# Router columns inside the first up unit's matmul group, and 12 of 64 recurrence slots as one instruction

## The chip, the cores and the metric

One core of one Trainium2 chip runs the whole program. The metric is the device time in microseconds (us) from the start to the end of one execution. The engines are TensorE (PE; its weight loads are listed apart as PEld), VectorE (DVE), ScalarE (ACT), GpSimd (POOL) and SyncE (SP), which only issues DMAs here.

## The reference

An image batch x of shape (8, 192, 16, 16) is taken as 8 sequences of 256 tokens with 192 channels. It passes two residual blocks:

```python
x = x + conv_ref(_ln_c(x), Wq, Wk, Wv, Wb, Wo)   # t = ln(x); returns t + delta_rule(...) @ Wo
t = tokens(x); t = t + ffn_ref(_ln_t(t), ...)
```

The first block is a delta rule with 12 heads of size 16. For each token, S is a 16x16 state per head, and with k and q normalised to length one

```
u_t = beta_t * (v_t - S_{t-1}^T k_t);  S_t = S_{t-1} + k_t u_t^T;  o_t = S_t^T q_t
```

The second block is a mixture of experts: a router gives 8 logits, of whose softmax the two largest are kept and normalised; each expert is silu(x @ w_gate) * (x @ w_up) @ w_down with a hidden size of 192, and a shared expert of hidden size 768 is mixed in by alpha = sigmoid(x @ sg_w + sg_b). All data are fp32.

## The kernel before, in words

**Chunks.** The 256 tokens of each sequence are cut into 16 chunks of T = 16 tokens; a chunk of 8 sequences has 128 tokens, one for each partition. All engines run the same outer loop `step(c)` for c from -3 to 18, and each writes out by hand, in one list for c < 1, one for 1 <= c < 16 and one for the rest, in which order it does its parts. `at(d, fn)` does the part fn for chunk c + d, so a step holds work of up to seven chunks:

- stage A of chunk c + 3 and c + 2 (norm, q, k, v projections, their silu and norms, splitting of k in a high and a low part, a trip through DRAM that lays k and q out for the recurrence),
- the recurrence of chunk c on DVE, with k rows put into PSUM by `fill(c, f)` on PE, two tokens at a time,
- `reading` and `summing` of chunk c on POOL: the products of states and q (`PQ`), half a chunk at a time, and their sums (`oT`),
- stage Fa of chunk c - 1: `Fa_otok` on DVE, `Fa_o` and `Fa_y` on PE (output projection and residual), norm, `Fa_h`, `Fa_hT` (the normed tokens transposed, high parts in `hiT`), `Fa_split` (low parts in `loT`), router logits, gates,
- stage Fb of chunks c - 1 and c - 2: 12 up units (8 experts, 4 quarters of the shared one). `Fb_up(n)` is five fp32r matmuls of 384 columns into one of two PSUM banks; ACT's `unit` makes `sg` (silu) and `ug` (times the gate) of them, POOL's `hidden` multiplies the two (`hid`), PE turns them by `Fb_turn(g)` in five groups, ACT copies them to `hidT`, `Fb_down(g)` multiplies them with the down weights,
- stage Fc of chunk c - 3 writes the output.

**The recurrence.** Each of a chunk's 16 tokens i takes four slots, 4i to 4i + 3: `Pr` = S * k (line 1301), `u` = minus the sum over a row of `Pr` (line 1303), k * u in place in PSUM (line 1305), and the new state `SH` (line 1309). In each slot a helper `each` issues the same operation twice, for the branches `br` 0 and 1 (six heads each, 128x96 elements); each branch waits for its own result of the slot before. Behind every slot `others(slot)` issues whatever small operations are hung on this slot by `at(slot, d, fn)`: stage A's and Fa's DVE parts and, at slots 48 to 58, the choice of the two experts (`Fa_max`, `G_dif`, ... `G_gate`).

**Router.** `Fa_logits` on PE is a plain fp32 product of `h2T` (an fp32 copy of the normed tokens, made by the last two of `Fa_hT`'s five ACT copies) with `Wr0`, `Wr1` into bank 1. DVE and ACT read the logits there.

**Start.** SP and ACT issue the loads of all weights. ACT and POOL split the up weights (`raw0`, `raw1`) into high and low parts in 12 pieces each (`weights_hi0`, `weights_lo0`, `weights_hi1`, `weights_1`). POOL's memsets come first of all; DVE builds `Sel` from `ident` after them, and PE waits for `Sel`.

## Time and profile before

| what | value |
|---|---|
| median of three runs | 497.47 us (497.37 to 498.15) |
| profiled execution, its own time | 497.98 us |
| its span, first to last instruction | 496.2 us |
| DVE busy | 428.0 us, 86% |
| PE busy | 425.9 us, 86% |
| POOL busy | 414.0 us, 83% |
| ACT busy | 349.7 us, 70% |

A busy share is the union of an engine's instructions over the span. The times in all rows count from the span's start. The steady part, chunks 2 to 12, lies between about 87 and 375 us; before it are the loads and the first chunks, behind it the last chunks and, from about 451 us on, the feed-forward work of the last two chunks.

### The profile page before, as it was taken

How to read it: one execution, taken by the hardware profiler on the slowest of the kernel's cores; microseconds unless marked ns; L12 is line 12 of the kernel's file. 1: busy time of each engine (PE TensorE's matmuls, PEld its weight loads, DVE VectorE, ACT ScalarE, POOL GpSimd, SP SyncE). 2: the span in 40 equal slices, each digit the busy share in tenths (PEclk: the TensorE clock that was granted, in tenths of full speed). 3: DMA queues.
4: the chain of work that ended last, by engine and by line, in shares of the span. 5: the costliest groups of instructions: out<-in, count | busy, mean ns of one | idle time of the engine just before them, and what ended most of it. 6: DMA issues, size and time to landing. Idle time of an engine off the chain costs nothing.

```text
span 496.2 us, 10722 instructions
## 1 busy us (share of the span) xinstructions
PE 425.9 (86%) x2464; PEld 391.3 (79%) x2464; DVE 428.0 (86%) x2546; ACT 349.7 (70%) x1039; POOL 414.0 (83%) x527
## 2 busy tenths in 40 slices
PE   0344276899999999999999999999999989899996
PEld 0233144789999989899898989898988979898996
DVE  2349989999999999999999999999999999997200
ACT  2795445686878787877778686878786848385763
POOL 5288699989899999999999898998999999896341
PEclk9855555999999999999999999999999999999999
DMA  7948373543323222323233332323222323200300
GB/s 203 223 100 159 94 180 100 111 103 111 79 68 88 72 78 74 92 65 102 68 84 87 81 89 78 89 72 83 80 83 74 83 78 86 81 28 0 114 2 16
DMA packets 44752, 44.12 MB, mean 89 GB/s; under 512 B 19920, under 2 KB 36496, under 8 KB 44688
## 3 DMA queue, kind: packets, MB, share of 16 engines
q1 hardware_dynamic: 40944, 40.87, 32.3%
q10 hardware_dynamic: 3744, 2.57, 1.8%
q8 instruction: 20, 0.33, 0.3%
q14 instruction: 44, 0.36, 0.2%
HBM read 37.13 MB, written 6.29 MB: 87 GB/s over the span
## 4 chain that ended last, share of the span: by engine, by line
DVE 73%; PE 11%; SPq 4%; issue 3%; POOL 3%; DMA 3%; ACT 2%; DVEq 0%; ACTq 0%; POOLq 0%
DVE Pr L1301 16%; DVE u L1303 15%; DVE bank L1305 15%; DVE SH L1309 12%; PE bank L427 2%; DMA k_scratch<-khl 2%; DVE st L1041 2%; SPq L249 2%; SPq L214 1%; DVE ss L1116 1%; PE bank L412 1%; DVE mv L1042 1%; DVE otok L1148 1%; DVE loT L1084 1%; PE bank L400 1%
## 5 line engine op out<-in xcount | busy, mean ns | idle before, releaser
L931 POOL TENSOR_TENSOR hid<-sg,ug 128x192 f32<-128x192 f32 x192 | 112.3, 608 | 23.0 <-ACT ug L669 21.4
L886 POOL TENSOR_TENSOR PQ<-SH,QB 128x768 f32<-128x768 f32 x62 | 112.5, 1835 | 5.8 <-DVE SH L1309 5.8
L1301 DVE TENSOR_TENSOR Pr<-SH,bank 128x96 f32<-128x96 f32 x512 | 104.8, 245 | 4.3 <-PE bank L361 3.9
L893 POOL TENSOR_TENSOR PQ<-PQ 128x768 f32<-128x768 f32 (+2 forms) x93 | 103.3, 1111 | 6.0
L1305 DVE TENSOR_TENSOR bank<-bank,u 128x96 f32<-128x96 f32 x512 | 106.5, 252 | 0.0
L427 PE MATMUL bank<-Wd,hidT 128*128 128x192 f32 x576 | 106.4, 326 | 0.0
L1303 DVE TENSOR_REDUCE u<-Pr 128x6 f32<-128x102 f32 x512 | 105.9, 247 | 0.0
L1309 DVE TENSOR_TENSOR SH<-SH,bank 128x96 f32<-128x96 f32 x512 | 103.0, 241 | 0.0
L427 PEld LDWEIGHTS bank<-Wd,hidT 128*128 128x128 f32 x576 | 95.3, 190 | 0.0
L668 ACT ACTIVATE sg<-bank 128x192 f32<-128x192 f32 x192 | 63.0, 328 | 45.0 <-PE bank L404 25.7
L361 PE MATMUL bank<-KR,Sel 128*128 128x384 f32 x128 | 58.3, 460 | 22.0 <-DVE SH L1309 12.5
L400 PE MATMUL bank<-Whi,hiT 128*128 128x384 f32 x192 | 72.2, 376 | 0.7 <-ACT ug L669 0.7
L404 PE MATMUL bank<-W,loT 128*128 128x384 f32 x192 | 65.3, 340 | 0.0
L402 PE MATMUL bank<-Whi,loT 128*128 128x384 f32 x192 | 65.3, 340 | 0.0
L403 PE MATMUL bank<-W,hiT 128*128 128x384 f32 x192 | 65.1, 339 | 0.0
L401 PE MATMUL bank<-Wlo,hiT 128*128 128x384 f32 x192 | 65.1, 339 | 0.0
L679 ACT ACTIVATE hidT<-bank 128x512 f32<-128x512 f32 (+1 forms) x80 | 44.3, 554 | 14.6 <-PE bank L412 12.8
L669 ACT ACTIVATE ug<-bank,gate 128x192 f32<-128x192 f32 x128 | 53.4, 417 | 0.0
L412 PE MATMUL bank<-ident,hid 128*128 128x128 f32 x288 | 45.7, 277 | 7.6 <-ACT hidT L679 7.5
L703 ACT ACT_TABLE_LOAD x38 | 48.8, 1283 | 0.7
L361 PEld LDWEIGHTS bank<-KR,Sel 128*128 128x128 f32 x128 | 25.9, 204 | 27.7 <-DVE SH L1309 16.6
L412 PEld LDWEIGHTS bank<-ident,hid 128*128 128x128 f32 x288 | 33.8, 141 | 12.4 <-issue 10.7
(150 smaller groups left out, 836.6 us busy)
## 6 DMA issues: line engine op xcount, KB each, us to landing
QB<-q_scratch SPq DMA_DIRECT2D x64, 384.0 KB
k_scratch<-khl SPq DMA_DIRECT2D x64, 48.0 KB, 1.7
KR<-k_scratch SPq DMA_DIRECT2D x32, 96.0 KB, 2.4
q_scratch<-qn SPq DMA_DIRECT2D x64, 24.0 KB, 1.6
Wd<-in_L_ffn_w_down_dram SPq DMA_DIRECT2D x4, 288.0 KB, 8.0
out_dram<-xT SPq DMA_DIRECT2D x1, 896.0 KB, 5.2
Wlo_unsplit<-in_L_ffn_w_gate_dram ACTq DMA_DIRECT2D x1, 768.0 KB, 5.6
Wlo_unsplit<-in_L_ffn_w_up_dram ACTq DMA_DIRECT2D x1, 768.0 KB, 8.8
```

The source lines that it names most:

```text
L361: mm(bKB[f % 2][:, 0:2 * BR * G], Sel[:, f].rearrange("p b x e -> p (b x e)"), KR[:, p, :], start=True, stop=True).then_inc(s_fill, 1)
L400: mm(to, hiT[:, p, 0:P], Whi0[:, n], start=True, stop=False)
L402: mm(to, loT[:, p, 0:P], Whi0[:, n], start=False, stop=False)
L412: last = tr(bHt[:, (k - lo) * P:(k - lo + 1) * P], hid[:, k % (KT // 2) * P:(k % (KT // 2) + 1) * P], ident[:, :])
L427: last = mm(bDn[:, 0:C], hidT[:, turn_half(g), k - lo, :], Wd[:, k, :], start=False, stop=(k == KT - 1))
L886: tt(PQ[:, at * BR * HP:(at + n) * BR * HP].rearrange("p (i b h) d -> p i b (h d)", i=n, b=BR), SH[:, lo:lo + n].rearrange("p i b h d -> p ...
L893: chained(tt(PQ[:, :, 0:w], PQ[:, :, 0:w], PQ[:, :, w:2 * w], ALU.add))
L931: tt(hid[:, r * H:(r + 1) * H], sg[:, m % RING], ug[:, m % RING], ALU.mult).then_inc(s_hid, 1)
L1301: v = each(lambda br: count(tt(Pr[:, br, i, :, 0:D], prev[:, br], KB[:, br], ALU.mult)), Sb)
L1303: v = each(lambda br: count(nc.vector.tensor_reduce(u[:, i % 2, br], Pr[:, br, i], X, ALU.add, negate=True)), v)
L1305: v = each(lambda br: count(tt(KB[:, br], KB[:, br], u[:, i % 2, br].unsqueeze(2).to_broadcast([P, HP, D]), ALU.mult)), v)
L1309: ins = tt(SH[:, i, br], prev[:, br], KB[:, br], ALU.add)
```

## The change

1. The router's columns stand ahead of unit 0's in the split weights. `Whi0`, `Wlo0` and `W1` get R = E + 2 = 10 columns in front (8 router columns and the shared gate's twice). `Fb_up(0)` multiplies 394 columns instead of 384; the logits are its columns 0 to 8 in `bUp[0]`. `Fa_logits`, `h2T` and its two copies, `Wr0` and `Wr1` go. DVE's `Fa_max` and ACT's `Fa_exp` read `bUp[0]`. Nine DMAs on SP load the router's columns instead of four.
2. In chunks 1 to 15, the slots of `WHOLE` (12 of 64) issue one instruction of 128x192 for both branches instead of two of 128x96; it waits for both.
3. `rstd_1` = 1 + rstd, a DVE operation in `A_bias`, becomes `A_plus` on ACT.
4. Waits at the start are moved: DVE's first wait for the memsets of `loT` and `hlo` goes to `A_low`, PE's wait for `Sel` to the first `fill`.
5. The written-out orders of PE, ACT, POOL and DVE are new. In both versions all 12 gated products of a chunk are done by POOL (`hidden`).

```diff
+R = E + 2
+WHOLE = frozenset((28, 32, 37, 38, 49, 50, 51, 54, 55, 56, 57, 58))
+        def columns(n):
+            return slice(0 if n == 0 else R + n * 2 * H, R + (n + 1) * 2 * H)
...
-                sp.dma_start(Wr0[:, 0:E], router_w[0:C0, :]).then_inc(s_wr, 16)
...
+                load_router(sp, 0, raw0[:, :], 0, C0)
+                load_router(sp, 1, raw1[0:C1], C0, C)
+                load_router(sp, 1, raw1[C1:P], C0, C)
...
-            def Fa_logits(f, p):
...
             def Fb_up(f, p, n):
-                to = bUp[n % 2][:, 0:2 * H]
-                mm(to, hiT[:, p, 0:P], Whi0[:, n], start=True, stop=False)
...
+                w = columns(n)
+                to = bUp[n % 2][:, 0:w.stop - w.start]
+                mm(to, hiT[:, p, 0:P], Whi0[:, w], start=True, stop=False)
...
             # PE, 1 <= c < 16
                     at(-1, Fa_h)
+                    at(-2, Fb_turn, 2)
+                    at(0, fill, 6)
                     at(-2, Fb_up, 11)
+                    at(-1, Fb_up, 0)
                     at(-2, Fb_down, 0)
-                    at(0, fill, 6)
-                    at(-1, Fa_logits)
-                    at(-2, Fb_turn, 2)
                     at(0, fill, 7)
-                    at(-1, Fb_up, 0)
+                    at(-2, Fb_down, 1)
                     at(-1, Fb_up, 1)
-                    at(-2, Fb_down, 1)
+                    at(1, fill, 0)
+                    at(-2, Fb_down, 2)
                     at(-2, Fb_turn, 3)
                     at(3, A_h)
...
             # ACT
+            def A_plus(a, p):
+                f(rstd_1[:, :], rstd1, ACT.Identity, bias=one[:, 0:1]).then_inc(s_plus, 1)
...
                 f(hiT[C1:P, p, P:2 * P], bFa[0:C1, P:2 * P], ACT.Copy)
-                f(h2T[:, 0:P], bFa[:, 0:P], ACT.Copy)
-                f(h2T[0:C1, P:2 * P], bFa[0:C1, P:2 * P], ACT.Copy).then_inc(s_h2T, 1)
...
                     at(-2, unit, 11)
+                    table(c + 2, LN_EXP)
+                    at(2, A_inv)
                     table(c - 1, LN_EXP)
                     at(-1, Fa_exp)
-                    table(c + 2, LN_EXP)
-                    at(2, A_inv)
                     table(0, SILU)
...
             # DVE
-                plus = count(ts(rstd_1[:, :], rstd1, 1.0, None, ALU.add))
-                dve.wait_ge(*plus)
...
             def Fa_max(q, p):
-                dve.wait_ge(s_lg, q + 1)
+                dve.wait_ge(s_up, q * UN + 1)
...
-                        at(8, 2, A_low)
-                        at(19, 2, A_z)
+                        at(7, 2, A_low)
+                        at(17, 2, A_z)
                         at(23, -1, Fa_otok)
-                        at(26, 3, A_stats)
-                        at(30, 3, A_var)
-                        at(30, 1, A_vT)
-                        at(31, -1, Fa_stats)
-                        at(31, -1, Fa_var)
-                        at(35, -1, Fa_bias)
-                        at(39, 3, A_bias)
-                        at(45, -1, Fa_split)
-                        at(46, 2, A_ss)
+                        at(27, 3, A_stats)
+                        at(28, 1, A_vT)
+                        at(31, 3, A_var)
+                        at(32, -1, Fa_stats)
+                        at(32, -1, Fa_var)
+                        at(36, -1, Fa_bias)
+                        at(37, 2, A_ss)
+                        at(38, 3, A_bias)
+                        at(43, -1, Fa_split)
                         at(48, -1, Fa_max)
...
-                            for br in range(BR):
-                                if waits[br] is not None:
-                                    dve.wait_ge(*waits[br])
-                                got.append(fn(br))
+                            for lo in range(BR) if c < 1 or slot not in WHOLE else (0,):
+                                hi = lo + 1 if c < 1 or slot not in WHOLE else BR
+                                for need in dict.fromkeys(made[lo:hi]):
+                                    if need is not None:
+                                        dve.wait_ge(*need)
+                                got += [fn(lo, hi)] * (hi - lo)
```

The other order changes that the text speaks of: POOL does `A_qn` before `A_vn` and `A_kn` and behind `hidden` 11; on ACT `A_h` and `A_xh` come behind the second table load, `unit` 1 ahead of `hidden` 3, and the last pieces `weights_hi1` behind `Fa_oc`; on PE `A_qk` comes ahead of `fill` 2 and `A_vb` behind it.

## Rows read from the trace of the kernel before

**Rows 1.** The page: the chain that ended last, shares of the span by engine.
```profile
DVE 73%; PE 11%; SPq 4%; issue 3%; POOL 3%; DMA 3%; ACT 2%; DVEq 0%; ACTq 0%; POOLq 0%
```

**Rows 2.** One steady chunk: busy us (count) of PE, PEld, DVE, ACT, POOL; clock; DMA.
```profile
237.28:263.41 26.13, 25.32 (x156) 23.88 (x155) 25.93 (x160) 20.51 (x64) 24.16 (x31) 1.00 0.31 81
```

**Rows 3.** The chain in order of time (start, us, what): one operation per chunk.
```profile
106.27 0.45 DVE ss L1116
...
367.92 0.45 DVE ss L1116
```

**Rows 4.** DVE's timeline in a steady chunk (start, us, line, operation).
```profile
236.67 0.27 DVE L1084 TENSOR_TENSOR loT<-bank,hiT 64x128 fp32r<-64x128 f32 x1
...
237.20 0.53 DVE L1116 TENSOR_REDUCE ss<-sq 128x24 f32<-128x384 f32 x1
237.66 0.40 DVE L1309 TENSOR_TENSOR SH<-SH,bank 128x96 f32<-128x96 f32 x2
...
238.33 0.16 DVE L1152 COPY logit<-bank 128x8 f32<-128x8 f32 x1
...
241.64 0.15 DVE L1194 RECIPROCAL rden<-den 128x2 f32<-128x2 f32 x1
241.71 0.40 DVE L1301 TENSOR_TENSOR Pr<-SH,bank 128x96 f32<-128x96 f32 x2
...
243.27 0.41 DVE L1301 TENSOR_TENSOR Pr<-SH,bank 128x96 f32<-128x96 f32 x2
243.60 0.41 DVE L1303 TENSOR_REDUCE u<-Pr 128x6 f32<-128x102 f32 x2
...
247.30 0.42 DVE L1301 TENSOR_TENSOR Pr<-SH,bank 128x96 f32<-128x96 f32 x2
...
253.07 0.37 DVE L1148 STREAM_TRANSPOSE otok<-oT 128x192 f32<-128x192 f32 x1
253.37 0.38 DVE L1301 TENSOR_TENSOR Pr<-SH,bank 128x96 f32<-128x96 f32 x2
...
254.32 0.35 DVE L1041 BATCH_NORM_STATS2 st<-bank 128x6 f32<-128x192 f32 x1
254.71 0.18 DVE L1042 BATCH_NORM_AGGREGATE mv<-st 128x2 f32<-128x6 f32 x1
...
260.31 0.14 DVE L1059 TENSOR_SCALAR rstd<-rs 128x1 f32<-128x1 f32 x1
260.49 0.21 DVE L1061 TENSOR_SCALAR nmr<-mv,rs 128x1 f32<-128x1 f32 x1
```

**Rows 5.** PE's timeline in that chunk.
```profile
237.09 0.36 PE L310 MATMUL bank<-Wr,h2T 128*128 128x9 f32 x2
...
237.70 0.66 PE L412 MATMUL bank<-ident,hid 128*128 128x128 f32 x4
...
239.27 0.34 PE L400 MATMUL bank<-Whi,hiT 128*128 128x384 f32 x1
...
240.14 1.46 PE L427 MATMUL bank<-Wd,hidT 128*128 128x192 f32 x8
...
246.71 0.42 PE L361 MATMUL bank<-KR,Sel 128*128 128x384 f32 x1
```

**Rows 6.** POOL's timeline in that chunk (in brackets the idle time before).
```profile
244.75 3.64 POOL L886 TENSOR_TENSOR PQ<-SH,QB 128x768 f32<-128x768 f32 x2 [0.30 <-DVE SH L1309]
...
252.06 0.37 POOL L910 TENSOR_TENSOR oT<-PQ 128x96 f32<-128x96 f32 x1
...
257.75 0.70 POOL L875 TENSOR_TENSOR rs<-ve,neg_half 128x2 f32<-128x2 f32 x1 [0.92 <-DVE ve L1071]
```

**Rows 7.** DVE's timeline in chunk 1: two of its waits.
```profile
59.71 0.42 DVE L1301 TENSOR_TENSOR Pr<-SH,bank 128x96 f32<-128x96 f32 x2 [0.74 <-PE bank L361]
...
73.49 0.36 DVE L1041 BATCH_NORM_STATS2 st<-bank 128x6 f32<-128x192 f32 x1 [0.69 <-PE bank L376]
```

**Rows 8.** The chain at the start: the first write of k to DRAM.
```profile
26.21 3.96 DMA k_scratch<-khl
```

More of the change, by code:

```diff
@@ L182, in later, with spare, unit_halves @@
             return n >= by
-        free = [b[:, i * 2 * H:(i + 1) * 2 * H] for b, n in (
-            (hid[:, :], 3), (sg[:, :, :].rearrange("p r h -> p (r h)"), 2), (ug[:, :, :].rearrange("p r h -> p (r h)"), 2),
-            (hidT[:, :, :, :].rearrange("p a k t -> p (a k t)"), 2)) for i in range(n)]
+        wide = R + 2 * H
+        free = [hid[:, 0:wide], hid[:, wide:wide + 2 * H], hid[:, wide + 2 * H:wide + 4 * H]] + [
+            b[:, i * 2 * H:(i + 1) * 2 * H] for b in (
+                sg[:, :, :].rearrange("p r h -> p (r h)"), ug[:, :, :].rearrange("p r h -> p (r h)"),
+                hidT[:, :, :, :].rearrange("p a k t -> p (a k t)")) for i in range(2)]
+        def spare(m):
+            return free[m % len(free)][:, 0:wide if m == 0 else 2 * H]
+        def unit_halves(m):
+            at = R if m == 0 else 0
+            return bUp[m % 2][:, at:at + H], bUp[m % 2][:, at + H:at + 2 * H]
         def turn_half(g):
@@ L482, in step @@
                     at(-2, Fb_turn, 4)
                     at(1, fill, 1)
-                    at(-1, Fb_up, 3)
+                    at(-2, Fb_down, 3)
                     at(-1, Fb_up, 4)
+                    at(3, A_qk)
+                    at(1, fill, 2)
                     at(3, A_vb)
-                    at(1, fill, 2)
-                    at(3, A_qk)
                 else:
+                    at(-2, Fb_up, 5)
                     at(-3, Fb_down, 4)
-                    at(-2, Fb_up, 5)
@@ L492, in step @@
                     at(-1, Fa_o)
+                    at(-2, Fb_up, 6)
+                    at(-2, Fb_up, 7)
+                    at(-1, Fa_y)
                     at(-2, Fb_turn, 0)
-                    at(-2, Fb_up, 6)
-                    at(-1, Fa_y)
-                    at(-2, Fb_up, 7)
+                    at(-2, Fb_up, 8)
+                    at(-2, Fb_up, 9)
                     at(-2, Fb_turn, 1)
-                    at(-2, Fb_up, 8)
                     at(-3, Fc_out)
-                    at(-2, Fb_up, 9)
+                    at(-2, Fb_up, 10)
@@ L658, in weights_hi1 @@
                     act.wait_ge(s_w1, m - len(free) + 1)
-                f(free[m % len(free)][C1:P].bitcast(F32R), raw1[C1:P, m], ACT.Copy).then_inc(s_whi, 1)
+                f(spare(m)[C1:P].bitcast(F32R), raw1[C1:P, columns(m)], ACT.Copy).then_inc(s_whi, 1)
             def unit(q, p, m):
@@ L742, in step @@
                     at(-2, unit, 3)
                     at(-2, unit, 4)
-                    at(3, A_xs)
+                    once(c, 1, weights_hi1, 7)
                     at(2, A_silu_qk)
-                    once(c, 1, weights_hi1, 7)
+                    at(2, A_sq)
+                    at(-3, Fc_res)
                     once(c, 1, weights_hi1, 8)
+                    at(0, place, 1)
+                    once(c, 1, weights_hi1, 9)
                     at(2, A_silu_v)
-                    once(c, 1, weights_hi1, 9)
@@ L1160, in G_dif @@
                 dve.wait_ge(*w["max"])
-                tt(table(slot, 0), bFa[:, 0:E].unsqueeze(1).to_broadcast([P, E, E]), logit[:, :].unsqueeze(2).to_broadcast([P, E, E]),
+                tt(table(slot, 0), bUp[0][:, 0:E].unsqueeze(1).to_broadcast([P, E, E]), logit[:, :].unsqueeze(2).to_broadcast([P, E, E]),
                    ALU.subtract).then_inc(s_nmx, 1)
@@ L1254, in others @@
                     else:
-                        at(3, -1, Fa_otok)
-                        at(14, -1, Fa_stats)
-                        at(18, -1, Fa_var)
-                        at(25, -1, Fa_bias)
-                        at(35, -1, Fa_split)
-                        at(35, -1, Fa_max)
+                        at(-1, -1, Fa_otok)
+                        at(0, -1, Fa_stats)
+                        at(24, -1, Fa_var)
+                        at(44, -1, Fa_bias)
+                        at(47, -1, Fa_split)
+                        at(48, -1, Fa_max)
                         at(48, -1, G_dif, done)
@@ L1313, in grow @@
                             return count(ins)
-                        Sb = state[:] = each(grow, v)
+                        Sb = state[:] = each(slot + 3, grow, v)
                         others(slot + 3)
```

241 lines of the change are left out of this document (119 added, 122 removed).

## The prediction

> **What bounds the kernel now.** I read the page of the profile first: of the span of 496.2 us the chain that ended last runs 73% on DVE and 11% on PE [rows 1]. Then the chain in order of time: from chunk 1 to chunk 11 one DVE operation comes back every (367.92 - 106.27) / 10 = 26.2 us, in a quiet chunk every 26.13 us [rows 2, 3], without a link on another engine that would show as a gap. The table by stretch says how near the others are: in 26.13 us DVE is busy for 25.93, PE for 25.32, POOL for 24.16 and ACT for 20.51 us, and PE has its full clock [rows 2]. PE's share is that of pipelined matmuls and overstates it, so the engine to fear behind DVE is POOL. Its timeline tells how near: it waits twice in a chunk, 0.30 us for the last state before `reading` 1 and 0.92 us for the variance before `rs` [rows 6]. The rest, 26.13 - 1.22 = 24.91 us, is work in one queue. So a DVE saving counts one to one for at most about 1.2 us a chunk, and less if it moves POOL's two waits against each other.
>
> DVE's timeline gives its price list [rows 4]. An instruction of 96 elements shows 0.245 us, but a pair follows the next pair after 0.33 us (243.27 to 243.60): 0.165 us from start to start. The reduction over 384 elements occupies 237.66 - 237.20 = 0.46 us, so an element costs (0.46 - 0.165) / 288 = 1.02 ns and each instruction some 0.067 us whatever its size. A two-element operation fits: 241.64 to 241.71, 0.07 us. An operation that needs the result just before it starts late: 192 elements start at 254.32, the one that reads them at 254.71, 0.39 us later. This is what the pairs hide: while branch 1 runs, branch 0's result lands.
>
> **The merged slots.** One instruction of 192 elements occupies 0.165 + 96 x 1.02 ns = 0.263 us instead of 0.33: 0.067 us saved, 12 times, 0.80 us in a chunk. The bound from the other side is the transpose of 192 elements, 0.30 us (253.07 to 253.37) [rows 4]: then only 0.03 x 12 = 0.36 us. I take 0.263, since the operation is of the kind of the pairs and the wide reduction, not a transpose. But now the next slot waits for this very instruction, 0.39 us behind its start. Where the order hangs a long enough operation in between nothing is lost: `A_vT`, `Fa_stats`, `A_ss`, `A_bias` behind slots 28, 32, 37, 38, the 64-element router operations behind 49, 50, 51, and `G_coef` behind 57. Behind 54, 55, 56 and 58 there is only an operation of 0.07 us: 0.263 + 0.07 = 0.333, so 0.055 us are waited. Slot 32 itself waits as much for slot 31's second branch. That gives back 5 x 0.055 = 0.28 us. Net 0.80 - 0.28 = 0.52 us a chunk.
>
> The page "Vector Engine (DVE) Microarchitecture Reference", section 5.2 on measured stream behaviour, in the Trainium skill, gives 1.0417 ns per column plus about 75 ns per instruction; by its figure the twelve instructions less would be worth 12 x 0.075 = 0.90 us, an estimate from that page, where my rows say 0.80. The page "VectorE: DVE Perf Modes", section on the DRAIN you can't avoid, says that after an operation the next does not start until the pipe is empty; by that every pair would take twice 0.245 us and a merger would save 0.145 us. The trace does not agree: the starts lie 0.165 us apart.
>
> **`rstd_1` off DVE.** It stands between 260.31 and 260.49, with the wait of its successor: 0.18 us [rows 4], in chunks 1 to 12. On ACT, which has 26.13 - 20.51 = 5.6 us free in a chunk [rows 2] and which loses the two `h2T` copies, it costs nothing.
>
> So DVE alone would come to 26.13 - 0.52 - 0.18 = 25.43 us.
>
> **What POOL makes of it.** `Fa_var` moves behind slot 32, 0.33 us later, while of the 0.70 us saved 0.63 lie behind it. The way from the variance to the end of slot 63 gets 0.33 + 0.63 = 0.96 us shorter; POOL had 0.30 us to spare there [rows 6], so it now begins `reading` 1 some 0.65 us late against DVE's slots. `oT` then ends 0.65 us later; before it ended at 252.43 and was read at 253.07 [rows 4, 6], so `Fa_otok` waits about 0.05 us. On the other side of the loop `rs` had 0.92 us and has 0.33 more. The loop closes at about 25.5 us rather than 25.43. I take 25.5: 0.63 us saved a chunk.
>
> **The router's columns.** On PE the four logits passes go, 237.70 - 237.09 = 0.61 us; an up unit is 240.14 - 239.27 = 0.87 us [rows 5], ten columns more make it 394/384 of that, 0.02 us. PE is not on the path in steady chunks, so this is worth nothing in itself. What matters is the latency: `Fa_max` needs all of unit 0. Before, `Fa_split`'s second operation starts at 236.67 and the logits are read at 238.33 [rows 4]. After, the split is behind slot 43 and `Fa_max` behind slot 48: 0.2 us for the rest of the split and five pairs of 0.33 us, 1.85 us. The path needs 0.27 us of split, 0.15 to PE (236.94 to 237.09), 0.89 of matmuls, of which the last shows 0.17 longer than its spacing: 1.5 us. That fits by 0.35 us, provided that PE stands at `Fb_up(0)`. Ahead of it are `fill` 6, free from slot 39's end, and unit 11, together 0.31 + 0.87 us against the 4 x 0.33 + 0.4 us until the split is done. It fits by about 0.5 us. In chunk 1 PE has the half clock, five matmuls take 1.6 us, and `Fa_max` waits some 0.4 us there.
>
> The price if the cover fails: PE's `fill` 1 ends at 247.13 and is read at 247.30 [rows 4, 5], 0.17 us to spare before. Its new place is behind two up units but before `Fb_down` 3 and no longer behind `fill` 0, which I reckon as even.
>
> **The sum.** Chunks 2 to 12: 11 x 0.63 = 6.9 us. Chunk 1: 0.63, and the wait of 0.69 us for `Fa_y` [rows 7] goes, as `Fa_stats` is a slot later and `weights_hi1` behind `Fa_oc`; less 0.4 for unit 0: 0.9 us. From chunk 13 on stage A's operations are missing, and merged slots stand bare: each costs its 0.39 against 0.33, so what is left is 0.2 us in chunk 13, 0.1 and nothing in the last two: 0.3 us. At the start `A_x` no longer waits for `Sel`, but the chain passes through the first write of k, which landed at 30.17 after 3.96 us [rows 8], behind the weights in the DMA queue, and then through DMAs until chunk 1 begins, which waits for its k rows [rows 7]; writing k 2 us earlier brings little, five more small DMAs on SP cost little: 0.2 us. At the end PE loses one logits pass: 0.3 us. Total 6.9 + 0.9 + 0.3 + 0.2 + 0.3 = 8.6 us. The profiled execution took 497.98 us, 1.8 more than its span; it would take 489.4. It lies 0.5 us above the median, so the median goes from 497.47 to 488.9 us; I say 489.0.
>
> **Rivals.**
>
> (a) The loops close late. POOL's lateness, unit 0 as a condition for `Fa_max`, or `fill` 1 holds DVE for another 0.3 to 0.45 us in every steady chunk, or the merged instruction takes 0.30 us (12 x 0.037 = 0.44 us a chunk). For: spare times of 0.17 and 0.30 us before. Against: everything that precedes the gates was also moved earlier. 8.6 less 11 times 0.3 or 12 times 0.45 leaves 5.3 or 3.2: 492 to 494.5 us.
>
> (b) Slower. One mechanism: PE is still in unit 11 when the split is done, so `Fb_up(0)` starts late, and DVE's queue stands at `Fa_max` with the recurrence behind it. It decides from a wait of more than 8.6 / 12 = 0.7 us a chunk at `Fa_max`, which needs PE 0.35 + 0.7 = 1.05 us late, a whole unit more than planned. Unit 11 would have to start only when the split is done; with a full unit and `fill` 6 behind that, 1.18 us late, the wait is 0.83 and the time 8.6 - 12 x 0.83 = -1.4: 499 us. PE's idle time in the chunk speaks against it.
>
> (c) More is gained. The start is not held by the DMAs: k is written 2 us earlier and all follows, and POOL does not bind (25.43 us): 8.6 + 1.8 + 11 x 0.07 = 11.2: 486.3 us.
>
> (d) Nothing: DVE's gain is wholly taken by POOL, whose loop stays at 26.1. Its 24.91 us of work speak against it: 497 us.
>
> **How the numbers follow.** Forecast (487.5 to 491) 0.58, (a) 0.21, (c) 0.12, (d) 0.03, (b) 0.06. The range takes in the forecast, most of (a), and (c): 486.0 to 494.0. A change of 0.2%, 1.0 us, is what a measurement here can tell. Faster by more: 0.58 + 0.21 + 0.12 = 0.91; same: 0.03; slower: 0.06.
>
> **What would show it.** 180 instructions of 128x192 in lines 1301 to 1309's groups, with 0.345 us each, and the next slot's start 0.263 us behind where something long is hung in between. The chunk's period at 25.5 us. No idle time before `logit`. POOL's 0.92 us before `rs` near 0.6, its 0.30 before `reading` 1 gone, and a short wait at `otok`. Chunk 1 beginning at 59.5. The prediction is wrong if DVE waits at `logit` for PE or for a `fill` in each chunk, or if the first states start 2 us earlier.

## The result, and the profile after

The changed kernel takes 494.34 us (median of 7 runs, 492.47 to 495.48), the kernel before 497.46 us beside it: ratio 0.9931, 95% interval 0.9912 to 0.9950. That is 3.1 us faster where 8.5 were forecast. Its profiled execution took 495.17 us, with a span of 493.4 against 496.2: the two traces differ by 2.8 us.

The page, busy time by engine and the chain that ended last:

```profile
PE 423.7 (86%) x2400; PEld 383.9 (78%) x2400; DVE 422.0 (86%) x2350; ACT 350.9 (71%) x1023; POOL 410.6 (83%) x527
...
DVE 70%; PE 13%; issue 5%; DMA 4%; SPq 4%; ACT 2%; ACTq 1%; POOL 0%; DVEq 0%; POOLq 0%
```

DVE still sets the time. The next two rows are from the table by stretch (columns as in [rows 2]): one quiet chunk (one without an irregular stall; these are treated further down), then chunks 2 to 12 together (a chunk is counted from its first `Pr` to the next chunk's).

```profile
191.85:217.60 25.75, 25.22 (x152) 23.25 (x151) 25.51 (x146) 20.58 (x63) 24.04 (x31) 1.00 0.31 85
...
88.36:373.08 284.72, 277.46 (x1636) 255.40 (x1635) 280.93 (x1597) 224.70 (x677) 264.05 (x330) 0.99 0.32 86
```

A quiet chunk is down from 26.13 us [rows 2] to 25.75, not to 25.5. And eleven times 25.75 is 283.3: chunks 2 to 12 hold 1.4 us more. DVE's timeline shows the merged instructions (those with 128x192, or 128x204 for `u`) in a quiet chunk:

```profile
204.05 0.36 DVE L1326 TENSOR_TENSOR Pr<-SH,bank 128x192 f32<-128x192 f32 x1
...
204.93 0.15 DVE L1091 TENSOR_SCALAR ve<-mv 128x1 f32<-128x1 f32 x1
205.00 0.41 DVE L1328 TENSOR_REDUCE u<-Pr 128x6 f32<-128x102 f32 x2
...
206.32 0.21 DVE L1097 TENSOR_SCALAR nmr<-mv,rs 128x1 f32<-128x1 f32 x1
206.51 0.37 DVE L1328 TENSOR_REDUCE u<-Pr 128x12 f32<-128x204 f32 x1
206.79 0.55 DVE L1138 TENSOR_REDUCE ss<-sq 128x24 f32<-128x384 f32 x1
...
212.07 0.21 DVE L1188 SCALAR_TENSOR_TENSOR eq<-bank,lower 128x64 f32<-128x64 f32 x1
212.20 0.35 DVE L1330 TENSOR_TENSOR bank<-bank,u 128x192 f32<-128x192 f32 x1
212.47 0.22 DVE L1193 SCALAR_TENSOR_TENSOR bank<-bank,eq 128x64 f32<-128x64 f32 x1
```

The merged instruction behaves as priced: 212.20 to 212.47, 0.27 us to the next start. What stands ahead of one does not. From the small `nmr` to the merged `u` pass 206.51 - 206.32 = 0.19 us; the same two steps unmerged take 0.12 (below).

In chunk 1, DVE's timeline has these waits:

```profile
60.53 0.42 DVE L1326 TENSOR_TENSOR Pr<-SH,bank 128x96 f32<-128x96 f32 x2 [1.54 <-PE bank L385]
...
69.58 0.38 DVE L1170 STREAM_TRANSPOSE otok<-oT 128x192 f32<-128x192 f32 x1 [0.56 <-POOL oT L932]
...
74.50 0.37 DVE L1063 BATCH_NORM_STATS2 st<-bank 128x6 f32<-128x192 f32 x1 [0.77 <-PE bank L400]
...
82.14 0.17 DVE L1174 COPY logit<-bank 128x8 f32<-128x8 f32 x1 [0.49 <-PE bank L422]
```

The wait for `Fa_y` (the row `st`), 0.69 before [rows 7], is not gone but 0.77. The wait at `logit`, forecast at 0.4, is there and in chunk 1 alone; later chunks have none. Chunk 1 takes 27.83 us (before 27.79) and begins at 60.53, not 59.5.

So, between the two traces: start +0.8 us, chunk 1 nothing, chunks 2 to 12 284.72 - 287.78 = -3.1, chunks 13 to 15 and the end -0.6.

### The profile page after: what moved, and what is told of

Its sections match the earlier page's. It is cut to its first block, busy times and chain, and to the rows that moved or that the text cites. A ratio compares the mean times of both kernels' runs of the same rounds, so it can differ in the third digit from the quotient of the medians.

```text
span 493.4 us, 10463 instructions
## 1 busy us (share of the span) xinstructions
PE 423.7 (86%) x2400; PEld 383.9 (78%) x2400; DVE 422.0 (86%) x2350; ACT 350.9 (71%) x1023; POOL 410.6 (83%) x527
## 4 chain that ended last, share of the span: by engine, by line
DVE 70%; PE 13%; issue 5%; DMA 4%; SPq 4%; ACT 2%; ACTq 1%; POOL 0%; DVEq 0%; POOLq 0%
DVE Pr L1326 15%; DVE bank L1330 15%; DVE u L1328 14%; DVE SH L1334 12%; PE bank L445 2%; DMA k_scratch<-khl 2%; SPq L237 2%; DVE st L1063 1%; PE bank L430 1%; PE bank L418 1%; SPq L272 1%; DVE otok L1170 1%; PE bank L422 1%; PE bank L420 1%; PE bank L421 1%
## 5 line engine op out<-in xcount | busy, mean ns | idle before, releaser
L1326 DVE TENSOR_TENSOR Pr<-SH,bank 128x96 f32<-128x96 f32 (+1 forms) x467 | 102.6, 256 | 10.1 <-PE bank L385 6.9
L1330 DVE TENSOR_TENSOR bank<-bank,u 128x96 f32<-128x96 f32 (+1 forms) x452 | 103.7, 268 | 0.1
L1328 DVE TENSOR_REDUCE u<-Pr 128x6 f32<-128x102 f32 (+1 forms) x467 | 103.5, 258 | 0.0
L1334 DVE TENSOR_TENSOR SH<-SH,bank 128x96 f32<-128x96 f32 (+1 forms) x482 | 102.9, 252 | 0.1
L418 PE MATMUL bank<-Whi,hiT 128*128 128x384 f32 (+1 forms) x192 | 80.5, 419 | 7.3 <-DVE loT L1104 6.4
L421 PE MATMUL bank<-W,hiT 128*128 128x384 f32 (+1 forms) x192 | 66.1, 344 | 0.0
L422 PE MATMUL bank<-W,loT 128*128 128x384 f32 (+1 forms) x192 | 66.1, 344 | 0.0
L420 PE MATMUL bank<-Whi,loT 128*128 128x384 f32 (+1 forms) x192 | 66.0, 344 | 0.0
L419 PE MATMUL bank<-Wlo,hiT 128*128 128x384 f32 (+1 forms) x192 | 65.9, 343 | 0.0
L418 PEld LDWEIGHTS bank<-Whi,hiT 128*128 128x128 f32 x192 | 37.0, 193 | 16.2 <-DVE loT L1104 9.8
```

The lines of the kernel that those rows point to most:

```text
L418: mm(to, hiT[:, p, 0:P], Whi0[:, w], start=True, stop=False)
L421: mm(to, hiT[:, p, P:2 * P], W1[:, w], start=False, stop=False)
L422: mm(to, loT[:, p, P:2 * P], W1[:, w], start=False, stop=True).then_inc(s_up, 1)
L1326: v = each(slot, lambda lo, hi: count(tt(Pr[:, lo:hi, i, :, 0:D], prev[:, lo:hi], KB[:, lo:hi], ALU.mult)), Sb)
L1328: v = each(slot + 1, lambda lo, hi: count(nc.vector.tensor_reduce(u[:, i % 2, lo:hi], Pr[:, lo:hi, i], X, ALU.add, negate=True)), v)
L1330: v = each(slot + 2, lambda lo, hi: count(tt(KB[:, lo:hi], KB[:, lo:hi], u[:, i % 2, lo:hi].unsqueeze(3).to_broadcast([P, hi - lo, HP, D]) ...
```

## Experiments on the merged slots

A merger is one instruction of 192 elements in place of a pair of 96. Two readings were open: the sum of the prediction (a merger saves what it was priced at), or that the merging itself is worth little, since what a merger saves is paid in waits around it. And the irregular 1.4 us may be chance, or belong to the program's code. The letters A and B in the expectations are each run's own. All ratios below are to the kernel before, run on the same chip.

**The same kernel again**, to see what repeats.

> The changed kernel once more, as the standard for the runs beside it. Ratio to before 0.993 (its first profile: 25.75 us in a quiet chunk, between 25.75 and 26.12 us in chunks 2 to 12, chunk 1 beginning at 60.53 us). Theory A (chance): the three chunks with 0.3 to 0.4 us more at slot 31 (2, 8 and 11) are accidents of that execution and lie elsewhere in this one. Theory B (schedule): they stand in the same chunks again, since the same work meets there.

Ratio 0.9926 [0.9906, 0.9946]. The quiet chunk is 25.72 us; six stalls lie at the same chunks and slots as in the first trace, equal to 0.01 us. They are no chance. Chunk 1 begins at 61.96 and takes 27.35 us instead of 27.83, with 0.14 us of wait for `Fa_y` instead of 0.77: the start and chunk 1 are not repeatable.

**No merging, and only six mergers.**

```diff
-WHOLE = frozenset((28, 32, 37, 38, 49, 50, 51, 54, 55, 56, 57, 58))
+WHOLE = frozenset()
```

```diff
+WHOLE = frozenset((28, 37, 38, 49, 50, 51))
```

> The changed kernel with an empty set of merged slots, all else the same: what are the mergers worth? Theory A (wait instructions and latency eat them; read from the slots of the changed kernel's trace, where slots 49 to 51 are shorter by 0.19 us, 53 to 58 longer by 0.08 us, 28 to 38 shorter by about 0.1 us): a quiet chunk takes 25.95 us, 0.2 more than the changed kernel, the whole kernel 2 to 3 us more, ratio to before 0.998 to 0.999. Theory B (the prediction's price, 0.52 us a chunk, and something else holds the chunk at 25.75): without the mergers a quiet chunk takes 26.2 to 26.3 us and the kernel is no faster than before, ratio 1.005 to 1.01.

> The changed kernel with six merged slots (28, 37, 38, 49, 50, 51) instead of twelve; slots 32, 54, 55, 56, 57, 58 are pairs again. Theory A (a merger with only a 0.07 us operation behind it, or with two waits ahead of it, costs as much as it saves or more): a quiet chunk takes 25.6 to 25.7 us, 0.05 to 0.15 less than with twelve, ratio to before 0.991. Theory B (each merger saves): 0.2 to 0.3 us more a chunk, 25.95 to 26.05 us, ratio 0.999.

Without mergers: ratio 0.9953 [0.9937, 0.9970], 1.2 us slower than with twelve. With six: 0.9865 [0.9844, 0.9885], 490.56 us. One quiet chunk of each, by the table by stretch:

```profile
217.03:242.88 25.85, 25.20 (x151) 23.25 (x151) 25.71 (x158) 20.50 (x63) 24.07 (x31) 1.00 0.28 81
```

```profile
111.92:137.50 25.58, 25.16 (x152) 23.31 (x151) 25.44 (x152) 20.53 (x63) 24.07 (x32) 1.00 0.34 96
```

Twelve mergers are worth 0.10 us a chunk, half of the 0.2 that the smaller of the two forecasts had; six of them are worth 0.27: the other six cost 0.17. DVE's timeline without mergers, the same places as above:

```profile
229.07 0.14 DVE L1074 TENSOR_SCALAR ve<-mv 128x1 f32<-128x1 f32 x1
229.15 0.42 DVE L1326 TENSOR_TENSOR Pr<-SH,bank 128x96 f32<-128x96 f32 x2
...
231.48 0.21 DVE L1097 TENSOR_SCALAR nmr<-mv,rs 128x1 f32<-128x1 f32 x1
231.60 0.41 DVE L1328 TENSOR_REDUCE u<-Pr 128x6 f32<-128x102 f32 x2
231.94 0.54 DVE L1138 TENSOR_REDUCE ss<-sq 128x24 f32<-128x384 f32 x1
```

Read slot by slot, from the first start of one to that of the next, the mergers save 0.05 to 0.065 us at the slots 28, 32, 37, 38, 49, 50, 51 and 57. They cost 0.133 ahead of slot 32, 0.061 ahead of 37, 0.053 ahead of 54, and 0.058 at 55, where nothing long covers the way to the next slot; 54, 56 and 58 come out even (the rest of the 0.10 are smaller shifts). Slot 32 alone, 0.133 against 0.063, is a loss.

**One wait instead of two.** An unmerged pair waits for branch 0's result, then for branch 1's. A merged instruction has both waits ahead of it, and the second implies the first when both count one semaphore.

```diff
-                                for need in dict.fromkeys(made[lo:hi]):
+                                needs = list(dict.fromkeys(made[lo:hi]))
+                                if len({id(q[0]) for q in needs if q is not None}) == 1 and None not in needs:
+                                    needs = needs[-1:]
+                                for need in needs:
```

> The changed kernel, but a merged instruction that follows a pair waits for the later of the two alone where both count on the same semaphore (slots 28, 37, 49, 54), so one wait instruction less before each. Theory A (a second wait costs about 0.06 us when the first is no longer hidden): slot 53 to 54 takes 0.46 instead of 0.52 us and slot 27 to 28 some 0.05 less, a quiet chunk 25.6 to 25.65 us. Theory B (waits that are already met are free, and slot 54 starts late for its data alone): nothing moves, 25.75 us.

Ratio 0.9883 [0.9864, 0.9902], quiet chunk 25.58. The slots ahead of 37 and 54 are 0.061 and 0.054 shorter, all of what the merger had cost there:

```profile
203.38 0.21 DVE L1097 TENSOR_SCALAR nmr<-mv,rs 128x1 f32<-128x1 f32 x1
203.51 0.35 DVE L1331 TENSOR_REDUCE u<-Pr 128x12 f32<-128x204 f32 x1
```

0.13 us instead of 0.19: a wait that was already satisfied costs DVE 0.06 us where the engine has nothing left to run. The wait ahead of slot 32 is on two semaphores and stays.

**Both edits together.**

> The kernel after, with mergers at the slots 28, 37, 38, 49, 50 and 51 alone, and one wait (for the later of the two) instead of two ahead of a merged operation. If the two edits add up (six mergers alone gave a quiet chunk of 25.58, one wait alone took 0.061 and 0.053 off the slots 36 and 53, of which 36 is in this one): quiet chunk 25.52 us, time 489.5 to 490.5. Rival: the pair ahead hides part of the wait, and the quiet chunk stays at 25.58.

Ratio 0.9878 [0.9847, 0.9909]. The quiet chunk is 25.49 (forecast 25.52), but the median is 492.0 where 489.5 to 490.5 were forecast, and the ratio lies between those of the two edits alone. This kernel has five stalls, 1.4 us in chunks 2 to 12, against two of together 0.62 with six mergers alone. That sent me to the stalls.

The stalls are only a part of it. In the traces of this run and of one_wait, chunk 14 takes 26.55 and 26.61 us; in the traces of the kernels after and with six mergers it takes 24.77 and 24.91. One wait in it, for `Fa_y`, is the difference; DVE's timeline and then the table by stretch, both of one_wait:

```profile
407.49 0.37 DVE L1063 BATCH_NORM_STATS2 st<-bank 128x6 f32<-128x192 f32 x1 [1.68 <-PE bank L400]
```

```profile
404.50:407.00 2.50, 2.50 (x9) 2.15 (x9) 1.18 (x7) 2.02 (x8) 1.89 (x4) 0.56 0.36 86
```

PE's granted clock is at the lower of its two levels there (0.56 as the mean of this stretch, 1.00 from 407.00 on; its passes of 384 columns follow each other after 0.32 us instead of 0.18), after PE had waited 1.55 us for `otok`. In the kernel after it waits 1.42 us at the same place and its clock stays at 1.00. Of the twenty traces only these two have it, and "best" below, which has the one wait too, does not; whether the edit or chance decides is open. So the two medians may hold up to 1.7 us that belong neither to the mergers nor to the stalls.

**The kernel before, with only the merging.**

> The kernel before, with the order, the router's separate product and the extra operations of before, and only the merging of the change, at the same twelve slots. Theory A (my step: a net 0.52 us a chunk is in the merging itself): the quiet chunk goes from 26.12 to 25.6 us and the time to about 492. Theory B (twelve mergers are worth 0.1 us, as leaving them out of the kernel after showed; with the order of before, other operations stand at other slots, so some mergers gain or lose another 0.1): the quiet chunk is 25.95 to 26.2 us and the time 495 to 498.

506.6 us, ratio 1.0173 [1.0143, 1.0202]: 1.7% slower, worse than either theory allowed. DVE's timeline at slots 36 to 39, with nothing hung in between:

```profile
289.89 0.41 DVE L1305 TENSOR_TENSOR Pr<-SH,bank 128x96 f32<-128x96 f32 x2
290.40 0.37 DVE L1307 TENSOR_REDUCE u<-Pr 128x12 f32<-128x204 f32 x1
290.81 0.37 DVE L1309 TENSOR_TENSOR bank<-bank,u 128x192 f32<-128x192 f32 x1
291.20 0.42 DVE L1313 TENSOR_TENSOR SH<-SH,bank 128x96 f32<-128x96 f32 x2
```

A bare merger costs on both sides: 0.51 us behind a pair where 0.33 are usual, then 0.41 and 0.39. The quiet chunk is 26.77, 0.65 more than before. So what the mergers give depends on the operations that the change hung at exactly these slots.

**`rstd_1` back on DVE** (`A_plus` gone, the operation of before in `A_bias`).

```diff
+                plus = count(ts(rstd_1[:, :], rstd1, 1.0, None, ALU.add))
+                dve.wait_ge(*plus)
                 ts(nmr1[:, :], mv1[:, 0:1], rstd1, -1.0, ALU.mult, ALU.mult).then_inc(s_nm1, 1)
```

> The kernel after, but one plus rstd is computed on VectorE in A_bias again, as before, with the product of A_bias waiting for it; A_plus is gone from ScalarE. Theory A (my step: the operation off VectorE is worth 0.18 us a chunk): the quiet chunk goes from 25.75 to 25.93 us and the time from 494.3 to about 496.7. Rival: the operation stood in a place where VectorE's pair needs no time of its own, and the quiet chunk stays within 0.05 us of 25.75 (time within 1 us of 494.3).

Ratio 0.9941 [0.9925, 0.9958]. The quiet chunk is 25.90: 0.15 us, so my term of 0.18 was about right. The ratio is only 0.1% above that of the kernel after; the trace shows why: this kernel has 0.3 us of stalls in chunks 2 to 12 instead of 1.4.

## Experiments on the irregular stalls

Take DVE's instructions of the trace, the separate waits (EVENT_SEMAPHORE) among them, number them from 0, and compare each chunk with its like. In the ten traces so far, every stall in chunks 3 to 12 begins at a number that is 63 (twice 62) modulo 128. Nearly always a separate wait stands at 60 to 62 (the expectations count two less, from the kernel's own first instruction), and the stall is 0.37 us at most. That is a condition, not a cause: in all twenty traces, chunks 3 to 12 have 102 such places and 31 of them show no stall that stands out, most of these with a wait at 62 alone; three stalls have their wait at 59. Whoever changes the number of instructions ahead moves all of them. So I added waits for a long past event ahead of chunk 0, where DVE is idle for 4 us:

```diff
                 else:
+                    for _ in range(10 if c == 0 else 0):
+                        dve.wait_ge(s_zero, 1)
                     others(-1)
```

(10 waits become 5 instructions; the second kernel has 78, which become 39.)

> The kernel after with ten more waits (for an event long past) on VectorE ahead of chunk 0, where it stands idle for four microseconds; they become five more instructions of VectorE, and nothing else changes. Theory B (the irregular stalls of 0.1 to 0.37 us come where a wait instruction of VectorE has a number of 58 to 60 in a block of 128 of its instructions; numbering them so explains all six stalls of the kernel after): with the numbers moved by five no wait instruction stands there, so chunks 2 to 12 take 11 x 25.75 + 0.03 = 283.3 us instead of 284.7, no chunk is longer than 25.8 apart from chunk 2 (26.1 less 0.37), and the time is 1.4 us less than the kernel after, about 492.9. Rival (the stalls come from other engines or memory traffic at those places of the chunks): they stay at the slots 31, 32 and 16 of the chunks 2, 5, 8, 9, 11, 12.

> The kernel after with 78 more waits on VectorE ahead of chunk 0, which become 39 more instructions. Theory B: the same rule puts thirteen stalls in chunks 2 to 12, of 0.35 us at chunk and slot (7, 32), (8, 63), (11, 17), (11, 63), (12, 47) and of 0.08 to 0.17 at (2, 17), (2, 63), (4, 32), (5, 17), (5, 63), (6, 47), (8, 17), (9, 47), 2.8 us in all: chunks 2 to 12 take 286.1 us and the time is 495.7. Rival: as with five, the stalls stay where they were in the kernel after and the time is 494.3.

The table by stretch, chunks 2 to 12, five more instructions and 39 more:

```profile
88.24:371.51 283.27, 276.86 (x1636) 254.97 (x1635) 280.66 (x1597) 224.82 (x677) 264.44 (x330) 0.99 0.31 86
```

```profile
88.62:374.66 286.04, 277.11 (x1637) 255.33 (x1636) 281.66 (x1596) 225.22 (x678) 264.88 (x330) 0.99 0.32 86
```

Forecast 283.3 and 286.1, measured 283.27 and 286.04. With five more there is no stall left, and the slots are otherwise equal to 0.02 us; with 39 more there are stalls at all thirteen forecast places, to within a slot, and one of 0.06 us that was not forecast. That this sum came out to 0.1 us is in part luck: single stalls are off by 0.12 us and more (three of the five forecast at 0.35 took 0.23, 0.23 and 0.28; two forecast at 0.08 to 0.17 took 0.22 and 0.23). Chunk 8, slot 31 in the kernel after, then with five more instructions:

```profile
255.93 0.35 DVE L1326 TENSOR_TENSOR Pr<-SH,bank 128x192 f32<-128x192 f32 x1 [0.44 <-ACT Pr L628]
256.20 0.36 DVE L1063 BATCH_NORM_STATS2 st<-bank 128x6 f32<-128x192 f32 x1
```

```profile
254.96 0.36 DVE L1328 TENSOR_TENSOR Pr<-SH,bank 128x192 f32<-128x192 f32 x1
255.23 0.36 DVE L1063 BATCH_NORM_STATS2 st<-bank 128x6 f32<-128x192 f32 x1
```

The view names a releaser for the 0.44 us, ACT's copy into `Pr`, and the second trace shows that it is not: the same copy is there, the wait is not. The medians, 494.27 and 495.53 beside 498.72 for the kernel before (ratios 0.9920 [0.9899, 0.9940] and 0.9945 [0.9926, 0.9963]), lie in the right order, but only 1.26 us apart where the stretches differ by 2.77; and the first is no better than the kernel after (0.9926 and 0.9931), where 1.4 us less were forecast. Starts that differ by 3 us between executions (below) can hide as much; that they do is not shown.

> Mergers at the slots 28, 37, 38, 49, 50 and 51 alone, and two more waits ahead of chunk 0, which become one more instruction of VectorE. Theory B: the two stalls of the kernel with six mergers (0.27 at chunk 8 slot 63, 0.35 at chunk 10 slot 31) go, two of 0.08 may come at slot 39 of chunks 4 and 12; chunks 2 to 12 take 281.5 us instead of 282.1 and the time is 490.0. Rival: 490.6 as without the shift.

The two stalls of 0.27 and 0.35 are gone, two of 0.09 came at the forecast chunks. But chunk 2 now loses 0.35 us, most of it in a wait for PE's `fill` 4 (more on it under v_early), so chunks 2 to 12 take 282.2 and not 281.5. Ratio 0.9866 [0.9848, 0.9884], as without the shift: no gain to be measured.

## Experiments on chunk 1 and the start

In the kernel after, in chunk 1, PE's timeline shows who is late:

```profile
69.93 0.45 PE L345 MATMUL bank<-ident,xs 128*128 128x128 f32 x1 [2.81 <-ACT v L599]
70.31 0.37 PE L346 MATMUL bank<-ident,xs 64*128 64x64 f32 x1
70.60 0.47 PE L337 MATMUL bank<-ident,otok 128*128 128x128 f32 x1
```

`A_x` waits for ScalarE's `v`, and `Fa_o` is queued behind it. `v` now stands behind the squares, `place` and two weight copies.

```diff
                     at(2, A_silu_qk)
+                    at(2, A_silu_v)
                     at(2, A_sq)
...
                     once(c, 1, weights_hi1, 9)
-                    at(2, A_silu_v)
```

> The kernel after, with ScalarE's silu of v moved ahead of the squares in chunks 1 to 15 (it stood behind the squares, the down group's copy, place and two weight copies). Theory A (in chunk 1, VectorE waits 0.77 us for y because TensorE's A_x, which waits for v, stands ahead of the turn of o): A_x of chunk 1 is done before VectorE's o is turned, the wait of st falls from 0.77 to under 0.2 us, chunk 1 takes 27.1 us instead of 27.83, the time falls by 0.6. Rival: the low clock of TensorE in chunk 1 alone makes y late (in the kernel before the same wait was 0.69), and chunk 1 takes 27.6 to 27.9; or the squares, now later, make ss at slot 37 wait in every chunk, and the time rises.

DVE's row in its chunk 1:

```profile
74.14 0.37 DVE L1063 BATCH_NORM_STATS2 st<-bank 128x6 f32<-128x192 f32 x1 [0.18 <-PE bank L400]
```

The wait is 0.18 where the first trace had 0.77, and chunk 1 takes 26.94 us, 0.89 less. PE no longer stands at `A_x` when `otok` comes: `Fa_o` starts 0.43 us behind `otok`'s start (69.81 to 70.24) and not 1.02 (69.58 to 70.60). So the edit does what it was meant to, but 0.89 us is the difference of two draws. The kernel after has 0.14 at this wait in its second trace, and in the nine traces of kernels with the twelve mergers and the old place of `v` (`rstd_1` on ACT) chunk 1 takes 27.35 to 27.85 us and the wait is up to 1.22. The shortest of them is 0.41 above v_early, and six_v_shift below, with the same edit, takes 27.30. So the edit is probably worth something in chunk 1; how much is open.

Chunk 2 loses 0.38 us in a wait for `fill` 4. That isn't shown to be a price of the edit: it goes with how long PE's passes of 384 columns still follow each other after 0.32 us, the lower level of its clock. In v_early they do so until 5.0 us into chunk 2. In six_shift_1, where `v` was not moved, and six_v_shift it is 4.8 us, and 0.29 and 0.25 are lost at the same slot; in two traces with 4.1 it is 0.07 and 0.08, in all with 3.8 or less nothing. The median, ratio 0.9920 [0.9904, 0.9936], can't tell so little.

**The start.** Four edits: the router's columns loaded last; one transfer instead of two for the shared gate's columns; the order up to chunk 0 of before; the rest of x loaded between k's first scratch and the wait for it.

```diff
-                load_router(sp, 0, raw0[:, :], 0, C0)
...
                 load_up(sp, 1, raw1[C1:P], C0, C)
+                load_router(sp, 0, raw0[:, :], 0, C0)
```

> The kernel after, with the nine small router loads issued behind the eight loads of the up weights of rows C0 to C on SyncE's queue instead of ahead of them. Theory A (the nine issues on SyncE, 6.8 us, make the start late): chunk 1 begins 0.8 us or more earlier than in the kernel after (60.5 and 62.0 in its two profiles) and the time falls to about 493.3. Rival (the start is set by the backlog of weights in the DMA engines or by ScalarE's copies, which wait for the same loads either way): chunk 1 begins at 60.5 to 62 and the time stays within 0.5 us of 494.3.

```diff
-            for at in range(E, R):
-                eng.dma_start(to[:, at:at + 1], sg_w[lo:hi, :]).then_inc(s_wu[i], 16)
+            eng.dma_start(to[:, E:R].unsqueeze(2), sg_w[lo:hi, :].unsqueeze(1).to_broadcast([hi - lo, R - E, 1])).then_inc(s_wu[i], 16)
```

> The kernel after, with the two columns of the shared gate loaded by one transfer instead of two, so six router loads instead of nine on SyncE. Theory A (the issues on SyncE's queue, 0.2 to 1.6 us each, delay all loads of weights behind them, and with them the start): the last up weights are issued some 1.5 us earlier than the 19.26 of the kernel after and chunk 0 begins up to 1 us earlier. Rival (the DMA engines are full until 28 us whatever the order of issue): chunk 0 begins at 34.3 to 36 as in the eleven profiles and the time stays within 0.4 us.

> The kernel after, with the order of all four engines' work up to chunk 0 as in the kernel before (one plus rstd put ahead of h in it). Theory A (the new order of the start costs the 0.8 us by which chunk 1 began later): chunk 1 begins at 59.7 or earlier and the time falls by 0.5 to 1 us against the kernel after on this chip. Rival (the nine router loads or chance set it, not the order): chunk 1 begins at 60 to 61 as the mean of the eleven profiles with the new order, 60.3, and the time stays within 0.4 us of the kernel after.

```diff
                 at(1, scratch_k)
+                if c == -1:
+                    load_later()
                 at(1, load_k)
```

> The kernel after, with the load of the rest of x on SyncE moved from behind the spread of q of chunk 0 to between the issue of k's scratch of chunk 0 and the wait for it (SyncE stands idle there for 5 us). Theory A (chunk 1 begins when KR of chunk 1 lands, and the issue of the rest of x, 5.7 to 7.5 us, stands ahead of it on SyncE): KR of chunk 1 is issued at 52 instead of 56.3, chunk 0 takes 24.5 us, and the time falls by up to 1.5 us. Rival (the traffic of x delays k's scratch of chunk 0 by as much): chunk 0 begins 1 us or more later than 34.4 and the time stays or rises.

> The kernel before, profiled once more. If the start is a fixed part of the difference (after has lost 0.8 us there), chunk 1 begins within 0.3 us of 59.7 again (59.3 in the kernel before with mergers alone, whose start is the same). If single executions differ as much as those of the kernel after and its relatives, where the same start put chunk 1 at 58.75 to 61.96, it lies anywhere in 58.5 to 62.

| kernel | chunk 0, chunk 1 begin | ratio |
|---|---|---|
| before; again; with mergers alone | 34.05, 59.71; 33.45, 60.48; 33.30, 59.30 | 1; 1.0006; 1.0173 |
| after; again | 34.42, 60.53; 36.00, 61.96 | 0.9931; 0.9926 |
| router last | 38.81, 63.56 | 0.9981 [0.9963, 1.0000] |
| six router loads | 34.73, 59.20 | 0.9937 [0.9915, 0.9959] |
| start in the old order | 35.63, 62.38 | 0.9932 [0.9908, 0.9956] |
| x between | 37.68, 62.16 | 0.9949 [0.9929, 0.9969] |

The router loads at the end are dear for another reason than I tested: ScalarE's first weight copy covers the router's columns and waits for them (ScalarE's timeline; in the kernel after this copy starts at 22.65 without a wait).

```profile
31.30 0.94 ACT L668 ACTIVATE Whi<-Wlo_unsplit 128x394 fp32r<-128x394 f32 x2 [8.49 <-DMA Wlo_unsplit<-in_L_ffn_sg_w_dram]
```

Fewer loads and the old order change nothing that can be measured. With x moved, k's second scratch leaves earlier (SyncE's rows, the kernel after, then x between), and chunk 0 takes 24.5 us instead of 26.1. The move alone is not shown to do that: with x in its old place chunk 0 took 24.4 to 24.6 us in six other traces too. And chunk 0 itself begins at 37.68, 1.7 us or more behind every other trace of the new kernels but router_last's (34.13 to 36.00), as the rival said; that the traffic of x delays k's first scratch was not looked at by itself.

```profile
38.19 5.66 SPq L272 DMA_DIRECT2D xT<-in_x_dram  x1
43.89 7.40 SPq L237 DMA_DIRECT2D k_scratch<-khl  x4
56.28 1.18 SPq L253 DMA_DIRECT2D KR<-k_scratch  x2
```

```profile
40.38 2.09 SPq L237 DMA_DIRECT2D k_scratch<-khl  x4
50.56 1.20 SPq L253 DMA_DIRECT2D KR<-k_scratch  x2
```

With the start of the kernel after, chunk 1 began at 58.75 to 61.96 in thirteen profiles (those with other edits behind it among them); with that of before, at 59.30 to 60.48 in three. So the 0.8 us between the two first traces is within what single executions differ by. Why one execution's issue of k's second scratch takes 4.9 us and another's 7.7 stays open.

**All together.**

> Three edits that the earlier runs point to, together: mergers at six slots (28, 37, 38, 49, 50, 51), silu of v ahead of the squares, one more instruction of VectorE ahead of chunk 0. By the sum: chunks 2 to 12 at 25.58 with 0.16 of stalls, 281.6 us, and up to 0.4 more in chunk 2, where TensorE is still at its low clock; chunk 1 at 26.8 to 27.0 instead of 27.7. The ratio to the kernel before is 0.985, between 0.983 and 0.987 for what single starts differ. If the edits take from each other, it is not under the 0.9866 of the six mergers with the shift.

> The same with one wait instead of two ahead of a merged operation (slot 36, 0.06 to 0.09 us a chunk), and the shift that suits its numbers (54 waits, 27 instructions; the rule puts 0.35 us at chunk 7 slot 32, 0.17 at (10, 31) and 0.08 at (12, 43)). By the sum the quiet chunk is 25.50 us, chunks 2 to 12 take 281.1 us plus up to 0.4 in chunk 2, and the ratio to the kernel before is 0.984.

Ratios 0.9854 [0.9834, 0.9874] and 0.9856 [0.9834, 0.9878], medians 491.09 and 491.25 beside 498.59. A chunk of the last (its chunks 2 to 12 take 281.43 us, chunk 1 26.08; of its three forecast stalls, 0.35, 0.17 and 0.08, the first took 0.22, the second 0.36, and the third did not come; six_v_shift's chunk 1 takes 27.30, not 26.8 to 27.0):

```profile
188.72:214.24 25.52, 25.07 (x152) 23.24 (x151) 25.38 (x152) 20.58 (x63) 24.08 (x31) 1.00 0.30 83
```

Both beat the kernel after by 0.7% and the kernel before by 1.5%; their intervals overlap with that of the six mergers alone, which is the edit that carries the gain.

## Why the prediction was wrong

The direction and the bound were right, the size was not. By the steps of the prediction:

- **The merged slots, net 0.52 us: the step that failed.** It is 0.10 us, which leaves 11 x 0.42 = 4.6 us ungained. The instruction itself was sized nearly right (0.27 against 0.263 us). What I missed stands ahead of it. I let slot 32 wait 0.055 us for the second branch of the slot before, and it pays 0.133 (with a separate wait of 0.06 the sum would be 0.115; its parts were not separated). The second wait instruction, 0.06 us ahead of slots 37 and 54, had no term at all; it was visible in the diff, where the loop waits for each need. The losses that I did charge came: 54, 56 and 58 are even as reckoned, 55 costs 0.058 more.
  The page "Vector Engine (DVE) Microarchitecture Reference" of the Trainium skill, section 5.2, puts about 75 ns on each instruction; the eight mergers that save anything save 50 to 65 ns, so the measurement stands a little below it. The page "VectorE: DVE Perf Modes" of the Trainium skill, section on the DRAIN you can't avoid, has the next operation wait for an empty pipe, but adds what the prediction left out: one that is not held starts earlier. The traces agree with this addition, if it takes in our operations, and not with the rule alone: a merged instruction that shows 0.35 us is followed by the next start after 0.27. The same section finds that a semaphore after every operation costs nothing extra; the one_wait run shows 0.054 to 0.061 us for a second, separate wait.
- **`rstd_1` off DVE, 0.18 us:** 0.15 on the chip. What remains of 26.13 - 25.75 = 0.38 us, 0.13, came with the rest of the change, by elimination the moved operations; I had no term for it. It was not separated further.
- **What POOL makes of it, 25.5 against 25.43:** wrong in detail, without effect. POOL waits 1.01 us before `rs`, not 0.6, and DVE never waits at `otok` in a quiet chunk. With the other edits the chunk comes to 25.49, POOL still waits 0.66 us or more before `rs` and DVE has no wait at `otok`, so POOL binds neither there nor at 25.75, and the 0.07 us charged for it were not due.
- **The router's columns:** right. No wait at `logit` but the 0.49 us of chunk 1 (forecast 0.4), so rival (b) is out. `fill` 1 is never late in a quiet chunk either.
- **The sum, 11 equal chunks:** the kernel after has 1.4 us of stalls in chunks 2 to 12 that depend on where DVE's instructions fall in blocks of 128; the kernel before has 0.36. That is 1.1 us of the miss, and it could not be read from the trace of before, which shows it only as two odd chunks.
- **Chunk 1, 0.9 us:** failed. I wrote that the wait for `Fa_y` goes since `Fa_stats` is a slot later. I had followed `weights_hi1` past `Fa_oc`, but not `A_silu_v` behind the squares and from there through `A_x` to `Fa_o` on PE. With `v` earlier, `Fa_o` no longer stands behind `A_x`, and chunk 1 took 26.94 us. How much of the 0.89 is the edit's is open: in its second trace the kernel after itself gained 0.44 in chunk 1 (27.35 against 27.79).
- **The start, 0.2 us:** neither shown nor refuted; single starts differ by up to 3 us. The rival that gained 1.8 us there, (c), did not occur.
- **Chunks 13 to 15 and the end, 0.6 us:** 0.6 measured.

The result is in rival (a)'s range, but by luck: none of the causes named there is the one found. It is not a loop that closes late and not a longer merged instruction, but waits around it, and stalls that no rival had. The bookkeeping: 8.6 forecast, less 4.6 (mergers), 0.3 (`rstd_1`), 1.1 (stalls), 0.9 (chunk 1) and 1.0 (start, a draw), plus 1.4 (moved operations) and 0.8 (POOL), is 2.9; the traces show 2.8. That it closes so well says little: the 1.4 is what was left over, and chunk 1 and the start differ from trace to trace.

## What to carry over

Before two instructions are made one, count the waits that it collects and look at what stands right ahead of it and right behind: it needs a covering operation on both sides, and one wait per semaphore. Mergers are worth having slot by slot, by measurement, since here six of the twelve together cost more than they gave. Before a difference between two traces is called the effect of an edit, look at how far two traces of one kernel lie apart at that place. And when a chunk of a regular loop is 0.1 to 0.4 us longer than the others at the same place in every execution, move the code by a few instructions before looking for a data wait.

## What was not expected of the hardware

- A separate wait instruction on DVE, for something already done, delays the instruction behind it by 0.054 to 0.061 us where it is not hidden by a running one.
- In all twenty traces (74 stalls in chunks 3 to 12), each irregular stall of DVE begins at its instruction number 63, or thrice 62, modulo 128. It is 0.06 to 0.37 us long, repeats from execution to execution, and disappears or moves when instructions are added far ahead. The profile's page of the kernel after lists a queue of kind "instruction" beside the data queues:

```profile
q14 instruction: 44, 0.35, 0.2%
```

  44 packets of together 0.35 MB are 8 KB each. The page "Advanced Engine Details and Errata" of the Trainium skill, section ISA Cache, has cache lines of 16 KB, 256 instructions; by that, 8 KB would be 128, which is the distance found here, and not 256. That the stalls have to do with the fetch of such a block would fit, and the traces have a sign of it: of the 421 times that DVE's instructions came to 63 modulo 128, an 8 KB packet of this queue begins within 0.5 us before to 1 us behind it 232 times; at numbers 0, 31 and 95 it is 33 to 41 of about 420. That the fetch causes the stall, and why it needs a separate wait just ahead, no run here shows.
- The profile can name a data releaser for such a stall (ACT's `Pr` above) that is not its cause.
